# PE's products with the old state for lane 0, issued in slot 0 of a step instead of slot 1

## What is computed

```python
q = l2norm(silu(conv4(x @ Wq))) * d**-0.5            # 8 heads of 128
k = l2norm(silu(conv4(x @ Wk)))                      # 3 x 8 heads
v = silu(conv4(x @ Wv))                              # 3 x 8 heads
beta = 2 * sigmoid(x @ Wb)
g = -exp(A_log) * softplus(x @ Wa + dt_bias)
for each token t:
    S = S * exp(g_t)
    for i in range(3):
        S = S + beta_i * k_i (v_i - k_i S)           # S is 128 x 128 for each head
    o_t = q_t S
x1 = layernorm(x + (rmsnorm(o) * silu(x @ Wg)) @ Wo)
out = layernorm(x1 + experts(x1))                    # top 2 of 8 experts
```

## Time and profile before

| | us |
|---|---|
| median of 3 runs | 8102.13 |
| lowest, highest | 8089.04, 8104.49 |
| the profiled execution | 8104.79 |
| its span, first to last instruction | 8103.0 |
| PE matmuls busy | 7272.4 (90%) |
| PE weight loads busy | 6184.4 (76%) |
| DVE busy | 6431.8 (79%) |
| ACT busy | 5452.1 (67%) |
| POOL busy | 4114.1 (51%) |

### The profile page before, as it was taken

The page is one execution under the profiler, slowest core; times in us unless marked ns, Lnnn a source line. Parts: engine busy times, 40 slices in busy tenths (PEclk is TensorE's granted clock), DMA queues, the critical chain, the costliest instruction groups (busy, mean ns, idle before and its releaser), DMA issues. The chain is left out here.

```text
span 8103.0 us, 425307 instructions
## 1 busy us (share of the span) xinstructions
PE 7272.4 (90%) x155940; PEld 6184.4 (76%) x155940; DVE 6431.8 (79%) x22300; ACT 5452.1 (67%) x20343; POOL 4114.1 (51%) x6333
## 2 busy tenths in 40 slices
PE   5899999989989898989898889898988989889999
PEld 3777777777777777777777777777777777767777
DVE  4888888888888888888888888888888888533333
ACT  3777777777777777777777777777777777433333
POOL 0555555555556555555555555555555555411111
PEclk6899999999999999999999999999999999899999
DMA  2000000000000000000000000000000000000000
GB/s 91 8 9 9 10 9 10 9 10 9 10 9 10 10 10 10 9 10 9 10 9 10 10 9 10 10 10 9 10 10 9 10 10 10 19 19 8 10 8 8
DMA packets 283508, 96.47 MB, mean 12 GB/s; under 512 B 226097, under 2 KB 276545, under 8 KB 281153
## 3 DMA queue, kind: packets, MB, share of 16 engines
q1 hardware_dynamic: 281408, 68.93, 3.9%
HBM read 52.08 MB, written 16.78 MB: 8 GB/s over the span
## 5 line engine op out<-in xcount | busy, mean ns | idle before, releaser
L823 DVE SCALAR_TENSOR_TENSOR CY<-PP,CWV,CY 128x128 f32<-128x128 f32 x4608 | 1588.2, 345 | 103.8 <-ACT CY L740 13.7
L823 DVE SCALAR_TENSOR_TENSOR CY<-PP,CWK,CY 128x128 f32<-128x128 f32 x4608 | 1584.0, 344 | 74.8 <-ACT CY L740 0.7
L1035 POOL TENSOR_TENSOR UM<-U,C 32x256 f32<-32x256 f32 x1536 | 1105.0, 719 | 119.6 <-POOL UM L1035 26.5
L1028 POOL TENSOR_TENSOR Y<-U,C 32x256 f32<-32x256 f32 x768 | 553.6, 721 | 1017.8 <-DVE UQ L916 977.7
L532 PE MATMUL PP<-XT,WV 128*128 128x131 f32 x3072 | 736.6, 323 | 259.0 <-DVE CY L823 226.2
L532 PE MATMUL PP<-XT,WK 128*128 128x131 f32 x3072 | 739.0, 323 | 253.8 <-DVE CY L823 253.7
L1008 POOL TENSOR_TENSOR S<-R,BETA 96x4 f32<-96x4 f32 x512 | 101.3, 198 | 1401.6 <-DVE R L876 1310.8
L740 ACT ACTIVATE CY<-PP,CWK 128x128 f32<-128x128 f32 x1536 | 565.4, 368 | 351.3 <-PE PP L532 339.0
L1241 ACT ACTIVATE HS<-PH,B1S 128x512 f32<-128x512 f32 x512 | 351.7, 687 | 608.1 <-PE PH L1160 608.1
L532 PEld LDWEIGHTS PP<-XT,WV 128*128 128x128 f32 x3072 | 476.8, 196 | 364.4 <-DVE CY L823 299.5
L812 ACT ACTIVATE KQ<-CY 128x128 f32<-128x128 f32 x2048 | 740.6, 362 | 7.8
(11 more groups left out here) (228 smaller groups left out, 18959.3 us busy)
## 6 DMA issues: line engine op xcount, KB each, us to landing
EX<-exd SPq DMA_DIRECT2D x768, 32.0 KB, 2.2
exd<-EXS SPq DMA_DIRECT2D x16, 512.0 KB, 2.7
XR<-in_L_attn_x SPq DMA_DIRECT2D x65, 64.0 KB, 1.9
XL<-in_L_attn_x SPq DMA_DIRECT2D x16, 256.0 KB, 2.9
XRES<-in_L_attn_x SPq DMA_DIRECT2D x64, 64.0 KB, 2.6
x<-X SPq DMA_DIRECT2D x64, 64.0 KB, 2.9
XI<-x SPq DMA_DIRECT2D x16, 256.0 KB, 2.9
out<-OUT SPq DMA_DIRECT2D x16, 256.0 KB, 2.3
```

The costliest lines, as they stand in the source:

```text
L823: dve.scalar_tensor_tensor(CY[:, m % RING], ptile(m)[:, s:s + P], taps_of(m)[:, s:s + 1], CY[:, m % RING], ALU.mult, ALU.add).then_inc(tap ...
L1028: pool.tensor_tensor(Y1[r, :, :], U[r, par, :, r], over(first[r, :], [BK, NHEAD, BK], 1), ALU.mult).then_inc(seed_sb, 1)
L1035: pool.tensor_tensor(UM[r, lv], U[r, par, :, r], over(merge[lv][r, :], [BK, NHEAD, BK], 1), ALU.mult).then_inc(made, 1)
```

## The change

In a step, PE issues `old_state(0)` behind the projection of slot 0 rather than behind that of slot 1. Between the two places lie the first level of the inversion and the projection of slot 1. `old_state(1)` stays in slot 4, and `k // 4` gives the lane in both cases.

```diff
                         if known(i, 0, NSC):
                             project(i, half, SLOTS * c + k)
-                        if k in (1, 4) and do_run:
+                        if k in (0, 4) and do_run:
                             old_state(k // 4, run, rs, rc)
                         if do_inv and k == 4:
                             invert(invn, 1 - par, INV_AT[k])
```

## The result

| | before | after |
|---|---|---|
| median of 5 runs, us | 8104.49 | 8149.52 |
| lowest, highest | 8089.04, 8120.97 | 8138.48, 8158.70 |
| the profiled execution | 8104.79 | 8158.70 |
| its span | 8103.0 | 8156.6 |
| mean granted clock | 0.960 | 0.952 |

A forecast was written before the change was run, and what follows sets the result against it. DVE's in-order stream was taken to bound the step. From the profiled 8104.8 us, -13.2 (quarter 0) and +4 (clock) gave 8095.6; with the median 2.7 under the profiled run, about 8093 us was forecast, range 8070 to 8114.

The forecast's parts named there:

- What bounds the step: Attention steps: DVE's in-order stream sets the pace; around the change DVE waits once, in slot 4, 0.59 us in quarter 0.
- The moved work and its semaphores: Lane 0's four products, behind slot 0's projection: nothing added, 0.35 us of slack in quarter 1, so no new wait.
- Quarter 0: DVE's slot 4 wait falls from 0.59 to 0.31 us in 47 steps: -13.2 us, between 0 and -27.7.
- Loop starts: The 15 steps where the loop body begins: order changes, PE's sum does not; 0 us, ends -4.5 and +15.
- Quarters 1 to 3: PE reaches slot 4 up to 0.23 us earlier, DVE's 0.31 us wait stays: 0 us, ends -57.7 and +18.6.
- The clock: Thinner PE work in slots 2 to 4 brings a few more low stretches: +4 us, ends -10 and +40.
- A: Whole kernel: the clock stays as it is and only quarter 0 counts; 8089 us, chance 0.22.
- B: Quarter 0: the advance is swallowed because ACT's own order is late, its SiLU stays put; 8102 us, chance 0.15.
- C: Other quarters: DVE's waits shrink too, or low stretches become fewer; 8070 us, chance 0.13.
- D: Ahead of slot 4, above all in quarter 2: thinner PE work lowers the clock in many more steps; 8130 us, chance 0.12.
- signs for "wrong": Profile after: DVE's 0.59 us unchanged, a PE wait before line 564, or clock below 0.96 with more 24.9 and 30.9 us steps.
- The rule that the prediction cited: PE's clock: only long idle gaps lower it, so a wait grown by a fifth does nothing; the prediction kept +4 us regardless.

The follow-up runs named there:

- q123_only: Kernel before with the products moved to slot 0 in quarters 1 to 3 only, quarter 0 in the old order; 8105.73 us, 1.0015 of before.
- start_only: Kernel before with the new order only in the 15 of 256 steps that begin the loop body; 8142.46 us, 1.0053 of before.
- q0_not_start: Kernel before with the new order in quarter 0 only, except in steps that begin the loop body; 8116.47 us, 1.0018 of before.
- pad2_before: Kernel before with two idle DVE copies added in slot 8 of quarter 0; 8138.84 us, 1.0048 of before.
- pad_after: Changed kernel with one idle DVE copy added in slot 8 of quarter 0; 8157.33 us, 1.0066 of before.
- pad_before: Kernel before with one idle DVE copy added in slot 8 of quarter 0; median 8151.59 us, 1.0062 of before.
- fill_before: Kernel before with two idle 128 x 128 PE products ahead of the inversion's level in slot 6 of each step; 8083.35 us, 0.9979 of before.
- fill13: Kernel before with two idle 128 x 128 PE products in slot 6 of quarters 1 and 3 only; 8151.73 us, 1.0065 of before.

## Why the prediction was wrong

- **What bounds the step**: right in part. DVE's stream sets the pace, and in an undisturbed step it waits as read. But the prediction left out the wait for line 581, 135.4 us before the change. An undisturbed quarter 3, which it took to be like the others, has 1.09 us of it, and the other quarters have it in steps with low clock alone. And what DVE waits for in slot 4 is the third level of the inversion (line 552), not the second join.
- **The moved work and its semaphores**: right. The products wait for nothing in their new place.
- **Quarter 0, -13.2 us**: right, 0.28 us a step, and 13.0 us less wait for line 552 in these steps. Each waypoint came within some 0.1 us, but for the new 0.53 us wait of slot 2, which was forecast as a bound of that projection and not as a wait.
- **Loop starts, 0 us**: right for the work at equal clock, wrong as a bound. The ends of -4.5 to +15 us priced the order, not the clock behind it; 15 steps with the new order decide over about 40 us, and half of that or more is lost in other steps.
- **Quarters 1 to 3, 0 us**: right. q123_only is 8 us above before (8097.35 us, timed beside it), with an interval (1.0002 to 1.0028) that just leaves out 1, and inside the ends of -57.7 to +18.6.
- **The clock, +4 us with ends at -10 and +40**: this is the step that failed. By the medians the term is 45.0 + 13.2 = 58 us, by the profiled executions 53.9 + 13.2 = 67 us, both beyond its upper end. The end was twenty-five more low stretches at 1.65 us each. The trace has 24 more in steps 16 to 254, so the count was met; but more of them were of the 10.2 us kind, which the price left out, and the excess of those steps grew by 76 us, 3.2 us for each stretch more. The place was wrong as well: the term was argued from the stretch ahead of slot 4. The low clock came at the loop starts and in slots 6 to 8 of quarters 1 and 3, which the edit does not touch.
- **Rivals**: A and B both would have given less than 8104 and are out. C is out. D had the right sign and the right kind of cause, 8130 us, with a chance of 0.12; its place was wrong in the changed kernel. Its signs for "wrong" were a mean clock under 0.96, which came (0.952), and longer quarters 1 and 2, which came for quarter 1 alone (+28.6 us; quarter 2 +4.0).
- **The rule that the prediction cited**: by the Trainium skill, TensorE: Matmul & The Clock Gate, section HAM oscillation, it is long idle gaps of PE that bring the clock down, and by that rule alone the time would have been rival A's 8089 us. The trace does not agree: in the step at 2377 us the longest wait of PE in the 5 us before the half-clock window at 2386.40 is 0.62 us. The measurement decides.

**What stays open.** Shown is that an edit in 15 steps (start_only) or in the quarters 0 alone (q0_not_start, pad2_before) moves the time through steps whose code is unchanged, and that the loss is time at low clock. Not shown is why the new order in the 15 loop starts costs some 40 us. The 10.2 us at 1.2 GHz behind a start are not the answer: start_only and pad_after had the loss with that stretch only once each. Whether the order counts there or merely the time it shifts is untested, since no run put idle work into those steps in the old order. Nor can I say before a run which of the two levels a step will meet.

## What to carry to other kernels

Where the granted clock is under 1 within a loop, an edit that shifts steps by a few tenths of a microsecond can change the time by the clock alone; here it cost up to some 0.6%. So give that term a range taken from how the iterations of the kernel before differ among themselves (here 424.7 to 435.6 us, with a mean of 428.6: 7 us more in each of 15 is an upper end of about 105 us, an estimate) and not from the edit, and put idle work of a known size into the kernel before, as pad_before, to see how far the time moves without any change of order. And look for the wait that only disturbed steps have: that is where denser work for PE may pay, as it did in fill_before (8083 us). It has to be measured, since the same work in two of the four quarters lost 49 us (fill13).

## What the runs showed of the hardware

- More work on PE made the kernel faster: two more 128 x 128 products a step, 0.60 us of its time, and 16 us less (0.9979). The mean clock rose from 0.960 to 0.968. The same two products in quarters 1 and 3 alone made it 49 us slower (1.0065).
- In 22 quarters 1 of the changed kernel the clock fell to 1.2 GHz in slots 6 to 8 with no PE wait over 0.62 us in the 5 us ahead; the rows above show levels of 48 matmul records of 32 x 32 there, with a projection between them. Ahead of the falls in the other quarters PE waited up to 1.1 us (before: 1.5 us).
- At the start of each loop iteration PE stands 2.9 to 5.0 us (3.40 before, 2.92 after in the rows above), and the half clock around it lasts from 3.4 to 10.2 us.
- One program took from 8106 to 8162 us in six runs (pad_before), the kernel before from 8083 to 8140 us in 22 runs, and 15 steps of 256 with the same instructions in another order changed the time by 0.5%.
